# One unread TensorE product ahead of the wait for the scans, at every second state, in a Mamba and mixture-of-experts kernel

## The reference

```
dt = softplus(dt @ dt_proj_w.T + dt_proj_b);  A = -exp(A_log)
h  = exp(dt_t[..., None] * A) * h + (dt_t * x_t)[..., None] * B_t[:, None, :]    # for each token t
y  = einsum('bdn,bn->bd', h, C_t)                                               # sum over the 16 states
y  = (y + xc * D_param) * silu(z);  out = y @ out_proj_w.T
```

## Time and profile before

| what | before |
|---|---|
| median of 3 runs | 5006.31 us (5001.06 to 5010.78) |
| profiled execution | 4998.19 us, span 4996.5 us |
| mean granted clock of TensorE | 0.952 |
| PE, PEld busy | 83%, 58% |
| DVE, ACT, POOL busy | 85%, 72%, 71% |
| DVE idle before L1217 until PE's L954 | 139.6 us, 112 times |
| PE idle before L954 until DVE's L1217 | 264.3 us for the MATMULs, 528.6 us for the LDWEIGHTS |

### The profile page before, as it was taken

The page is one execution under the profiler, slowest core; times in us unless marked ns, Lnnn a source line. Parts: engine busy times, 40 slices in busy tenths (PEclk is TensorE's granted clock), DMA queues, the critical chain, the costliest instruction groups (busy, mean ns, idle before and its releaser), DMA issues. The chain is left out here.

```text
span 4996.5 us, 76410 instructions
## 1 busy us (share of the span) xinstructions
PE 4150.0 (83%) x21374; PEld 2881.0 (58%) x21374; DVE 4243.0 (85%) x6062; ACT 3574.0 (72%) x6537; POOL 3565.3 (71%) x2235
## 2 busy tenths in 40 slices
PE   2688888888888888888888888888888889888886
PEld 1455555555656665565566656566665566655663
DVE  3899999988999988899988889899888888878752
ACT  3677767777776777777777777777777777776753
POOL 3676677666666667777777777778787886777853
PEclk7899999999999999999999999999998999999988
DMA  5122222243343424333333433333354453555653
GB/s 131 41 85 85 91 87 75 85 145 102 113 138 123 125 91 122 100 105 106 95 103 84 122 102 104 104 96 105 82 145 114 125 132 92 163 141 141 177 154 86
DMA packets 348420, 552.00 MB, mean 110 GB/s; under 512 B 39377, under 2 KB 196178, under 8 KB 347874
## 3 DMA queue, kind: packets, MB, share of 16 engines
q1 hardware_dynamic: 279026, 448.92, 29.8%
q0 software_dynamic: 47616, 65.17, 6.4%
q10 hardware_dynamic: 21360, 33.03, 1.8%
HBM read 432.78 MB, written 181.33 MB: 123 GB/s over the span
## 5 line engine op out<-in xcount | busy, mean ns | idle before, releaser
L587 POOL TENSOR_TENSOR dBx<-dtx,Bbc 128x1024 f32<-128x1024 f32 x1024 | 2445.1, 2448 | 439.9 <-DVE hs L1201 425.6
L1201 DVE TENSOR_TENSOR_SCAN hs<-ps,dBx 128x512 f32<-128x512 f32 x2048 | 2406.6, 1207 | 268.6 <-ACT ps L741 168.5
L741 ACT ACTIVATE ps<-dt,A 128x512 f32<-128x512 f32 x2048 | 1396.2, 689 | 476.4 <-DVE hs L1201 453.5
L954 PE MATMUL ps<-ident,hs 128*128 128x128 f32 x8192 | 1297.3, 292 | 389.1 <-DVE acc L1217 264.3
L954 PEld LDWEIGHTS ps<-ident,hs 128*128 128x128 f32 x8192 | 976.5, 148 | 912.3 <-DVE acc L1217 528.6
L1217 DVE SCALAR_TENSOR_TENSOR acc<-ps,C_tok,acc 128x512 f32<-128x512 f32 x1664 | 1184.1, 734 | 150.7 <-PE ps L954 139.6
L622 POOL DMA_INDIRECT X_slots<-xs,slots x248 | 248.0, 1000 | 356.1 <-DVE slots L1339 295.9
L643 POOL DMA_INDIRECT fx<-Y_slots,slots x248 | 392.4, 1582 | 143.8 <-issue 48.9
L919 PE MATMUL ps<-xnT,w_in 128*128 128x512 f32 x512 | 266.7, 636 | 86.8 <-DVE xc L1190 57.2
L1190 DVE SCALAR_TENSOR_TENSOR xc<-ps,conv_w,xc 128x511 f32<-128x511 f32 (+2 forms) x384 | 284.8, 742 | 61.3 <-ACT xc L705 53.3
L1113 PE MATMUL ps<-xsT,wx 128*128 128x128 f32 x2432 | 312.1, 280 | 16.8 <-ACT xsT L833 15.9
(11 more groups left out here) (209 smaller groups left out, 6262.6 us busy)
## 6 DMA issues: line engine op xcount, KB each, us to landing
Bbc<-B_scratch SPq DMA_DIRECT2D x512, 256.0 KB, 3.8
wx<-in_experts SPq DMA_DIRECT2D x304, 384.0 KB, 3.9
Y_slots<-zeros SPq DMA_DIRECT2D x228, 256.0 KB, 4.4
xin<-X_slots SPq DMA_DIRECT2D x304, 128.5 KB, 3.0
Y_slots<-xin SPq DMA_DIRECT2D x304, 128.0 KB
xt<-in_x SPq DMA_DIRECT2D x32, 512.0 KB, 5.2
shared<-xt ACTq DMA_DIRECT2D x31, 512.0 KB, 3.1
fx<-shared SPq DMA_DIRECT2D x31, 512.0 KB, 4.5
```

The costliest lines, as they stand in the source:

```text
L587: pool.tensor_tensor(dBx[u % 3][:], dtx[b % 2][:, 2 * h:2 * h + 2, :], Bbc[g % NBB][:, n % CH:n % CH + 1, :].broadcast_to([P, 2, T]), ALU. ...
L741: act.activation(psA[s % 2][:], dt[b % 2][:, j, :], ACT.Exp, scale=A[:, j, n:n + 1]).then_inc(s_dA, 1)
L954: i = pe.transpose(psH[w % 2][:, j * P:(j + 1) * P], hs[(n * CT + j) % NHB][:, t * P:(t + 1) * P], ident[:])
L1201: dve.tensor_tensor_scan(hs[s % NHB][:], psA[s % 2][:], dBx[s // 2 % 3][:, s % 2, :], 0.0, ALU.mult, ALU.add).then_inc(s_scan, 1)
```

## The change

At the first group of every even state, PE makes one matrix product with the identity as weights and the first 256 columns of the weight tile w_m2 as the moving operand. It writes columns 0 to 255 of the PSUM bank that the transposes of this group fill next, and nobody reads it: the first two transposes overwrite these columns. It stands behind the wait that frees the bank and ahead of the wait for the four scans. It has no semaphore of its own. There are 8 of them in a batch, 256 in all. Its form is that of the product at L1000, `pe.matmul(psG[q][:, t * D:(t + 1) * D], ident[:], x[:, 2 * q + t, :], ...)`, with D = 256.

```diff
@@ -949,6 +949,8 @@
                     yield w // (NS * NTB)
                     if w >= 2:
                         pe.wait_ge(*weighs((w - 2) // (NS * NTB), (w - 2) // NTB % NS, (w - 2) % NTB))
+                    if t == 0 and n % 2 == 0:
+                        pe.matmul(psH[w % 2][:, 0:256], ident[:], w_m2[:, 0, 0:256], start=True, stop=True)
                     pe.wait_ge(s_scan, n * CT + CT)
                     for j in range(CT):
                         i = pe.transpose(psH[w % 2][:, j * P:(j + 1) * P],
```

## The result

| | before | after |
|---|---|---|
| median of 9 runs each, in turn on one chip | 5010.78 us | 5056.90 us |
| lowest and highest | 4995.75, 5038.75 | 5036.93, 5071.35 |
| profiled execution's span | 4996.5 us | 5037.2 us |
| mean granted clock in it | 0.952 | 0.960 |

The ratio is 1.008, 95% interval 1.0053 to 1.0107: the kernel became slower by 40 us (27 to 54). Forecast was +30 us, a ratio of 1.006.

The account below looks back on a forecast made before the run. Bound: a loop of DVE scans, PE transposes and DVE weighings, DVE most loaded. Delays 43 plus 4 at half clock, less 17 from the clock, gave +30: 4998.19 to 5028, plus 8.1 for the median, 5036 us; range 4988 to 5085.

Parts of the forecast that it names:

- state 0: Batch start: PE has no pause until L1113 ends, DVE's L1351 waits; 0.44 us passes, uncharged in the first six batches.
- state 2: First four transposes end 0.30 us before DVE takes them up, so 0.14 us of the product passes.
- state 4: DVE had been idle 3.23 us for just these four transposes, so 0.44 us passes.
- state 6: First four transposes have slack, but DVE already waited a little for the next, behind L1035; 0.40 us passes.
- state 14: The weighing behind is late by 0.4 us, but DVE then idles 1.30 us for ACT's decay; nothing passes.
- states 8, 10 and 14: Places with visible cover, from waits for DVE, ACT's slack or DVE's stop on ACT; nothing passes.
- state 12: 0.2 us reach DVE, but waits behind it, with DVE's 1.41 us stop, leave nothing surviving at full clock.
- Return predicted: Products before clock falls remove 85 us of low clock, worth 0.2 a us: 17 us back.
- The 85 of the prediction: Low clock that might go, of 255 us between 230.1 and 4476.3; about one fall in three has a product before it.
- faster rival: Products hold the clock nearly everywhere; 255 us at 0.26 gives 66 back against 47: -19, 4987 us; chance 0.2.
- No change: PE's idle time or DVE's stops on ACT absorb nearly all, clock's 17 against some 20; about 5008 us; chance 0.2.
- Much slower: Every product delays DVE, also in a batch's second half: 113 - 17 = +96, so 5102 us; chance 0.15.

Follow-up runs that it names:

- e4_behind: Against the changed kernel, the same 256 products moved behind the wait for the scans, directly ahead of the transposes; ratio to the kernel before 1.0080.
- e9_state_15: Against the changed kernel, the product at state 15 alone (32 of 256); ratio to the kernel before 0.9957, 22 us below it.
- e2_covered: Against the changed kernel, products at states 8, 10 and 14 alone (96 of 256); ratio to the kernel before 0.9998.

## Why the prediction was right

**Price and cover.** A product holds PE 0.43 us, as priced from L1000. That PE does not wait for the scans at even states is shown by e4_behind: 249 of 256 found them done. The prediction's 792.9 us of idle PE were MATMULs and LDWEIGHTS added up, 264.3 for the MATMULs; its sum does not use them.

**The eight states.** Predicted and read in DVE's stream in batches with the full clock: state 0, 0.44 and 0.38; state 2, 0.14 and 0.16; state 4, 0.44 and 0.43; state 6, 0.40 and 0.43; state 14, taken back, and it was (0.47 and -0.47). Over the 25 batches from the seventh on the medians of the first four are 0.38, 0.16, 0.42 and 0.38. The runs with the first four places and with states 8, 10 and 14 bear out the division (34 us and 0). Two points were off. State 0's delay does not reach DVE through the expert's L1351, as I wrote, but earlier, through the transposes of the sums into L1253 (0.29 of idle at 1512.66, none before); PE and DVE are then late by the same amount and L1353's stop does not grow. And state 12, booked at nothing, sets DVE back by 0.3 us at the full clock and by over 1 us where the clock is low: the stop of 1.41 us that was to absorb it is itself fed through PE's line and does not always take it back. It did in the batch shown (1.12 late at 1622.20, and no stop before the scan pair at 1624.64); in others it gave back 0.21 of 0.30, or nothing.

**The sum.** Charged: 47 us. Measured at an equal clock: 1.84 us a batch from the profile, 59 in 32 batches, or 57 from the runs. The terms were further off than their sum. Read from the runs at an equal clock, the four places charged 47 cost 36, states 8, 10 and 14, booked at nothing, 12, and state 12, booked at nothing too, 9 (from the profiles 37, 15 and 16 to 18). One error went against the other. At the half clock the products that could be read took 0.85 to 1.05 us of PE, where 0.88 was taken.

**The clock.** Return predicted: 17 us. The profile's low time is 2 x 0.048 x 4996.5 = 480 us before and 2 x 0.040 x 5037.2 = 403 after, 77 us less. The 85 of the prediction was meant for the stretch from 230.1 to 4476.3, and there it fell from 280 to 236 us only, 44 less (53 in the 30 batches; the rest of the 77 went at the two ends). At 0.29 and not 0.2 a us the 53 give 15 us; from the runs it is 15 to 20. So the return of 17 was met by luck: the low time that goes was put too high by more than half and its worth too low by a third. I had taken the worth from two early batches, but the early ones are not the cause: a line through batches 1 to 6 alone has a slope of 0.30 for after, one through the later ones 0.29. That later batches pay more, as the faster rival had it, is not borne out, and neither is its other half, that nearly all low time would go.

So +47 - 17 stood for about +58 - 18: two terms right in kind, the first a fifth too small, and each of the two put together from parts whose errors partly cancel. The mechanism, a cost set by what stands behind each place, is shown; the closeness of the sum is in part luck.

**The rivals.** Faster: refuted here (the low time of the stretch fell by 44 and not by 255), though its mechanism, a product that holds the clock, is at work in e9_state_15. No change: refuted. Much slower: refuted by the sum, and at states 8, 10 and 14 by e2_covered, where 12 to 15 us passed of 41 added. That PE would not fill a wait for the scans: shown.

## What to carry to other kernels

Added work on an engine in a coupled pipeline costs by its place: lay the most loaded engine's stream over that of the old kernel and look at which stops follow the added work directly, since twice the work cost three times as much here and half of it at other places nothing. Filler that is to keep the clock up belongs into a wait that it fits into with room to spare, in front of the gap after which the clock is seen to fall; one product there, in 32 batches, went with 22 us less where eight a batch lost 40. Before comparing kernels whose time differs by less than one per cent, read their runs both as measured and at an equal clock: the first has what a change does to the clock in it, the second only what it does to the work.

## What the runs showed of the hardware

- The spread of one kernel's runs goes with the clock: 24 us (before) and 36 us (after) for 0.01 of mean granted clock, 20 to 37 over all kernels, with 2 to 4 us of scatter around the line.
- A us at 1.2 GHz instead of 2.4 costs this kernel 0.2 to 0.3 us (eleven of the thirteen rows of the table; 0.13 to 0.31 over all).
- Four float32 transposes of 128 columns and a float32 product of 256, put in the same places, cost this kernel the same (1.0075 and 1.0080) and move the clock alike (means 0.957 and 0.956, before 0.950).
- Adding PE work does not raise the clock by its amount: with 512 columns in place of 256 the profile's mean clock is 0.961 against 0.960. Whether a small change can lower it (0.9463 for a single product at state 4 against 0.9495, 1.7 standard errors) stays open.
